# Uneven groups of tokens in a two-layer transformer kernel: groups of 8x6, 6, 6 and 4 units, with scatters, pieces and gathers set closer to each group's plan

## What is computed

```python
h = _layernorm(x) * (1 + ca) + sa
x = x + ga * attention(h)                  # 16 heads, softmax over 256 keys
h = _layernorm(x) * (1 + cb) + sb
topk_w, topk_i = jax.lax.top_k(h @ router_weight, 2)
# every token: only its two experts count
#   layer 0: act = (clip(up) + 1) * gate * sigmoid(1.702 * gate), with biases
#   layer 1: act = silu(h @ wg) * (h @ wu), plus a shared expert
x = x + gb * (w0 * expert_a(h) + w1 * expert_b(h))
```

## Time and profile before

| what | us |
|---|---|
| median of 3 runs | 1867.87 (1864.94 to 1874.45) |
| profiled execution, device time | 1869.03 |
| its span in the trace | 1867.3 |
| PE busy | 1491.6 |
| DVE busy | 1315.7 |
| ACT busy | 1157.5 |
| POOL busy | 1028.7 |

### The profile page before, as it was taken

One profiled execution on the slowest core, in us unless ns is written; L12 is line 12 of the kernel. 1 busy time (PEld: TensorE's weight loads), 2 busy tenths in 40 slices (PEclk: granted clock), 3 DMA queues, 4 the chain that ended last, 5 costly groups with the idle time before them and its releaser, 6 DMA issues.

```text
span 1867.3 us, 44529 instructions
## 1 busy us (share of the span) xinstructions
PE 1491.6 (80%) x13810; PEld 911.5 (49%) x13810; DVE 1315.7 (70%) x3981; ACT 1157.5 (62%) x2692; POOL 1028.7 (55%) x1411
## 2 busy tenths in 40 slices
PE   2779888889999888899999989998999887435540
PEld 1334444445555555555555555555555555435530
DVE  5669988978888877798888888887788765202110
ACT  1478877877777676677776767766776654113320
POOL 1223335634553766567764767565755556546736
PEclk9989999999999898899999999999999999667665
DMA  6774444445555554455554545555455433224432
GB/s 197 172 205 109 110 103 116 114 122 126 134 130 120 138 132 114 119 127 140 134 137 109 134 122 144 130 124 116 125 134 129 116 87 83 75 80 132 121 93 62
DMA packets 381606, 229.44 MB, mean 123 GB/s; under 512 B 28847, under 2 KB 370161, under 8 KB 380867
## 3 DMA queue, kind: packets, MB, share of 16 engines
q1 hardware_dynamic: 352675, 186.72, 41.4%
q0 software_dynamic: 16384, 33.59, 6.4%
q10 hardware_dynamic: 12320, 6.29, 1.2%
HBM read 122.44 MB, written 103.98 MB: 121 GB/s over the span
## 4 chain that ended last, share of the span: by engine, by line
PE 36%; POOL 20%; DVE 18%; issue 16%; another core or an unknown queue 4%; ACT 4%; DMA 2%; SPq 1%; POOLq 0%; DVEq 0%; ACTq 0%
DVE mx L1553 8%; PE ps_s L1161 7%; POOL y_in L642 7%; PE ps_job L1032 6%; PE ps_q L1020 3%; PE ps_q L1001 3%; POOL slot_dram L625 3%; PE ps_q L983 2%; POOL qk_part L669 2%; POOL y_two L677 2%; POOL qk_rest L665 2%; PE ps_job L1135 2%; PE ps_job L1127 2%; PE ps_q L1013 2%
## 5 line engine op out<-in xcount | busy, mean ns | idle before, releaser
L1553 DVE TENSOR_REDUCE mx<-ps_s 128x2 f32<-128x512 f32 x1024 | 688.2, 681 | 150.3 <-PE ps_s L1161 123.7
L821 ACT ACTIVATE prob<-ps_st 128x512 f32<-128x512 f32 x1024 | 598.9, 593 | 111.1 <-PE ps_st L1167 82.6
L1161 PE MATMUL ps_s<-k_stk,q_stk 51*128 51x256 bf16 x2048 | 403.4, 284 | 79.5 <-DVE mx L1553 37.2
L1167 PE MATMUL ps_st<-q_stk,k_stk 53*128 53x256 bf16 x2048 | 400.2, 281 | 0.8 <-ACT prob L821 0.8
L642 POOL DMA_INDIRECT y_in<-y_dram,slot x256 | 252.4, 986 | 106.7 <-issue 54.6
L1032 PE MATMUL ps_job<-prob,v_ext 128*32 128x256 f32 x4096 | 287.8, 400 | 25.6 <-issue 17.6
L625 POOL DMA_INDIRECT slot_dram<-h_row,slot x256 | 260.6, 1018 | 69.8 <-issue 65.1
L1161 PEld LDWEIGHTS ps_s<-k_stk,q_stk 51*128 51x128 bf16 x2048 | 118.3, 95 | 333.8 <-issue 182.7
L754 ACT ACTIVATE o_sb<-ps_job 128x256 f32<-128x256 f32 x256 | 97.1, 379 | 190.3 <-PE ps_job L1032 127.0
L1032 PEld LDWEIGHTS ps_job<-prob,v_ext 128*32 128x32 f32 x4096 | 115.1, 112 | 133.4 <-issue 54.4
L665 POOL TENSOR_TENSOR qk_rest<-qk_f,qk_part 128x512 f32<-128x512 f32 x64 | 73.9, 1154 | 187.3 <-ACT qk_part L852 187.3
(11 more groups left out here) (206 smaller groups left out, 2919.0 us busy)
## 6 DMA issues: line engine op xcount, KB each, us to landing
part_dram<-qk_part SPq DMA_DIRECT2D x128, 192.0 KB
q_stk<-part_dram SPq DMA_DIRECT2D x128, 192.0 KB
k_stk<-part_dram SPq DMA_DIRECT2D x128, 192.0 KB
...
part_dram<-qk_part SPq DMA_DIRECT2D x128, 128.0 KB
...
part_dram<-qk_part SPq DMA_DIRECT2D x128, 64.0 KB
```

Source lines behind the costliest of these rows:

```text
L821: sc.activation(prob[:, (k ^ 1) % 8, :], ps_st[k % 2][:], ACT.Exp).then_inc(exp_done, 1)
L1161: mm = pe.matmul(ps_s[j % 2][:, t * S:(t + 1) * S], q_stk[us.tri][r0:r0 + R_BIAS, hp, t * P:(t + 1) * P], k_stk[us.tri][r0:r0 + R_BIAS, hp ...
L1167: mm = pe.matmul(ps_st[k % 2][:, t * S:(t + 1) * S], k_stk[ut.tri][r1:r1 + R_MAX, hp, t * P:(t + 1) * P], q_stk[ut.tri][r1:r1 + R_MAX, hp, ...
L1553: dve.tensor_reduce(mx[:, hp // 4, :, 4 * par + hp % 4], ps_s[j % 2][:].rearrange("p (t s) -> p t s", s=S), AX_X, ALU.max).then_inc(max_do ...
```

## The change

- The units are split into groups of 8, 8, 8, 8, 8, 8, 6, 6 and 4 units. A group of 6 has 40 blocks (10 pieces), one of 4 has 32 (8 pieces): 100 pieces in all, not 96. There are 9 plans, not 8. The plan works on the group's own number of rows.
- The steps of scatters, pieces and gathers after a group's last unit change as in the table. Scatters and gathers of groups 0 to 4 take half as many steps as before.

| counted from | what | before | now |
|---|---|---|---|
| `last` | scatters of groups 0 to 5 | 91 to 181 | 92 to 138 |
| `last` | pieces of groups 0 to 4 | 195 to 312 | 147 to 264 |
| `last` | gathers of groups 0 to 4 (before: 0 to 4, one unit per 16 steps) | 332 to 450 | 286 to 348 |
| `END` | group 5: pieces, gathers | -61 to 56, 124 to 155 | -109 to -21, -2 to 36 |
| `END` | group 6: scatters, pieces, gathers | -37 to 53, 92 to 158, 176 to 207 | -68 to -34, -11 to 43, 58 to 81 |
| `END` | group 7: scatters, pieces, gathers | 91 to 122, 164 to 230, 248 to 279 | 31 to 54, 56 to 92, 107 to 130 |
| `END` | group 8: scatters, pieces, gathers | none | 90 to 105, 112 to 140, 152 to 167 |

- `slot_dram` has 3 buffers instead of 2. They are cleared by 18 DMAs of 512 KB, one every 10 steps from step 40 on, not by 2 of 3072 KB.
- Pieces of groups 6 to 8 (`quick`) go through their stages in 9 steps instead of 15.
- The gathers of groups 6 to 8 use four buffers: the two of `y_in` and two in the memory of `k_stk[0]`. Their gate rows come in two DMAs at `END+47` into the memory of `v_ext`, and DVE instead of POOL multiplies by them and adds to `x` (`add_rows`).

The core of the diff:

```diff
-G = 8
-NG = UNITS // G
-NB = G * S * 2 // P + E
+SIZES = [8] * 6 + [6, 6, 4]
+G = max(SIZES)
+NG = len(SIZES)
 QB = 4
+UNIT_AT = [sum(SIZES[:g]) for g in range(NG + 1)]
+BLOCKS = [size * S * 2 // P + E for size in SIZES]
+PIECES = [n // QB for n in BLOCKS]
 TAIL = NG - 2
+LATE = TAIL - 1
+RING = 4
...
-    for i in range(G):
+    for n in range(2 * TT * SIZES[g]):
+        SCATTER[last + 92 + n * 3 // 2 if late < 2 else END + (31, 90)[late - 2] + n] = (UNIT_AT[g] + n // 4, n % 4)
+    for i in range(PIECES[g]):
+        QUAD[last + 147 + 32 * (i // 3) + (0, 11, 21)[i % 3] if late < 0 else
+             END + (-109 + 8 * i, -11 + 6 * i, 56 + 4 * i, 112 + 4 * i)[late]] = PIECE_AT[g] + i
+    for i in range(SIZES[g]):
+        first = last + 286 + 8 * i if late < 0 else END + (-2 + 5 * i, 58 + 4 * i, 107 + 4 * i, 152 + 4 * i)[late]
+        apart, lag = (2, 13) if late < 0 else (1, 9)
         for j in range(2 * TT):
...
+STAGE = {"blocks": (0, 0), "gate_up": (3, 3), "clip": (3, 3), "tanh": (5, 3), "act": (6, 3), "product": (7, 7), "act_t": (10, 6),
+         "down": (15, 9), "store": (16, 10), "load": (-12, -5)}
...
+        y_rows = [y_in[0][:], y_in[1][:], spare[:, 0], spare[:, 1]]
+        gate_late = [v[:].rearrange("p t h v -> p (t h v)").rearrange("p (u d) -> p u d", d=D) for v in v_ext]
...
+                if step == END + 47:
+                    sp.wait_ge(av_mm, 4 * UNITS)
...
                     if u.no < 2:
                         pool.wait_ge(row_stored, 32)
+                    elif u.no < UNIT_AT[LATE] + 2:
+                        pool.wait_ge(y_summed, u.count(2, -2))
+                    elif u.no < UNIT_AT[LATE] + RING:
+                        pool.wait_ge(st_mm, S_DONE)
                     else:
-                        pool.wait_ge(y_summed, u.count(2, -2))
+                        pool.wait_ge(y_summed, u.count(2, 2 - 2 * RING))
...
-                if step == 40:
-                    clear_slots()
+                if step in range(40, 40 + 10 * 3 * CLEAR, 10):
+                    clear_slots(*divmod((step - 40) // 10, CLEAR))
...
+            def add_rows(u):
+
+                dve.wait_ge(y_summed, u.count(2, 2))
+                dve.wait_ge(gates_in, 32)
+                dve.wait_ge(sh_added, u.count1(1, 1))
+                i, j = divmod(u.no - UNIT_AT[LATE], 8)
+                dve.tensor_tensor(y_two[:], y_two[:], gate_late[i][:, j].rearrange("p (o d) -> p o d", o=1)
+                                  .broadcast_to([P, TT, D]), ALU.mult).then_inc(y_scaled, 1)
+                dve.wait_ge(y_scaled, u.count(1, 1))
+                dve.tensor_tensor(x[:, u.batch, :, :], x[:, u.batch, :, :], y_two[:], ALU.add).then_inc(y_added, 1)
```

More of the change, by code:

```diff
@@ L35 @@
 VW = 32
-G = 8
-NG = UNITS // G
-NB = G * S * 2 // P + E
+SIZES = [8] * 6 + [6, 6, 4]
+G = max(SIZES)
+NG = len(SIZES)
 QB = 4
-NQ = NB // QB
+UNIT_AT = [sum(SIZES[:g]) for g in range(NG + 1)]
+BLOCKS = [size * S * 2 // P + E for size in SIZES]
+NB = max(BLOCKS)
+PIECES = [n // QB for n in BLOCKS]
+PIECE_AT = [sum(PIECES[:g]) for g in range(NG + 1)]
+SECOND = UNIT_AT.index(B)
 TAIL = NG - 2
+LATE = TAIL - 1
+RING = 4
 LANES = 3
@@ L62, in __init__ @@
         self.batch = no - B * self.layer
-        self.group, self.slot = no // G, no % G
-        self.last = self.slot == G - 1
+        self.group = max(g for g in range(NG) if UNIT_AT[g] <= no)
+        self.slot = no - UNIT_AT[self.group]
+        self.last = no + 1 == UNIT_AT[self.group + 1]
     def count(self, per, c):
@@ L79, in __init__ @@
         self.no = no
-        self.group, self.i = no // NQ, no % NQ
-        self.layer = 0 if self.group < NG // 2 else 1
-        self.tail = self.group >= TAIL
-        first = TAIL * NQ
+        self.group = max(g for g in range(NG) if PIECE_AT[g] <= no)
+        self.i = no - PIECE_AT[self.group]
+        self.layer = 0 if self.group < SECOND else 1
+        self.quick, self.tail = self.group >= LATE, self.group >= TAIL
+        first = PIECE_AT[TAIL]
         self.par = no % 2
@@ L247, in build @@
         start_of = sb("start_of", [P, G * TT * 2])
-        slot = [sb(f"slot{i}", [P, G * TT * 2], U32) for i in range(NG)]
+        slot = [sb(f"slot{i}", [P, n * TT * 2], U32) for i, n in enumerate(SIZES)]
         over = sb("over", [NB, E])
@@ L310, in build @@
         zeros_in = sem("zeros_in")
-        slots_clear = sem("slots_clear")
+        slots_clear = [sem(f"slots_clear{i}") for i in range(3)]
         lanes_clear = sem("lanes_clear")
@@ L380, in act_done, with stored @@
             return (act0_ok, q.no + 1) if q.layer == 0 else (act_ok, q.count1(1))
+        def stored(g, n):
+            return (sum(PIECES[h] for h in range(g % 2, g, 2)) + n) * 16
         def y_freed(q):
@@ L505, in quad_store @@
                 sp.wait_ge(y_ok, q.no + 1)
+                if q.i == 0 and q.group >= 3:
+                    for par in range(2):
+                        sp.wait_ge(y_gathered[par], UNIT_AT[q.group - 2] // 2 * 64)
                 sp.dma_start(y_dram[q.group % 3].rearrange("(j p) d -> p j d", p=P)[:, q.i * QB:(q.i + 1) * QB, :],
@@ L527, in _ @@
                         max_rows(u, half)
-                q = quad_at(step, 16)
+                q = quad_at(step, "store")
                 if q:
                     quad_store(q)
-                q = quad_at(step, -12)
-                if q and q.i and not q.tail:
+                q = quad_at(step, "load")
+                if q and (q.i or q.quick):
                     quad_load(q)
-                q = quad_at(step, -5)
-                if q and (q.i == 0 or q.tail):
-                    quad_load(q)
+                if step + 6 in QUAD:
+                    q = Quad(QUAD[step + 6])
+                    if q.i == 0 and not q.quick:
+                        quad_load(q)
                 u = at(step, 44)
@@ L601, in count_seen @@
                     pool.wait_ge(rank_dn_mm, u.no)
-                    pool.wait_ge(seen_step, u.group * (G - 1) + u.slot)
+                    pool.wait_ge(seen_step, u.no - u.group)
                 if u.slot == 0:
@@ L673, in _ @@
                 u = done_at(step, 2)
-                if u:
+                if u and u.group < LATE:
                     pool.wait_ge(y_summed, u.count(2, 2))
@@ L1447, in plan @@
                 c = u.group * PLAN
+                n_blocks, n_rows = BLOCKS[u.group], SIZES[u.group] * TT * 2
+                mine, rows = hot_start[:, 0:n_rows, :], start_of[:, 0:n_rows]
                 if u.group:
@@ L1622, in _ @@
                     norm_rows(u)
-                if step == END + 66:
+                if step == END + 50:
                     dve.wait_ge(av_mm, 4 * UNITS)
@@ L1629, in _ @@
                     combine(u)
+                    if u.group >= LATE:
+                        add_rows(u)
 def kernel(**inputs):
```

150 lines of the change are left out of this document (81 added, 69 removed).

## The result

| | before | changed |
|---|---|---|
| median, us | 1867.7 (1864.94 to 1874.45) | 1822.0 (1816.94 to 1825.56) |
| ratio | | 0.9751, 95% interval 0.9719 to 0.9783 |
| span of the profiled execution | 1867.3 | 1820.1 |
| last unit begins (END) | 1494.5 | 1543.2 |
| last `slot` | 1603.7 | 1710.2 |

The account below looks back on a forecast made before the run. It took order stage by stage as the bound, chiefly the 263 us tail hanging on POOL's row of DMAs. END at 1531.5 (1494.5 - 7 + 26 + 28 - 10), then 151 and 99.5 us, gave 1782, forecast as 1783; range 1735 to 1840.

Parts of the forecast that it names:

- rival 2: Burst units lose 1 to 1.5 us each as scatters before `ln_rs` delay DVE: +40 to +55 us, 1820 to 1840; chance 0.2.
- clearing: ACT's queue: 18 small clears replace the big clear's 10.73 us hold; -7 us, bounds -11 and +2.
- END to last `slot`: From the last unit's start to the last plan: more pieces and a load wait, 151 us, bounds 109 and 170.
- after the last `slot`: Tail behind the last plan: scatters, gathers beside the last pieces, final gathers; 99.5 us instead of 263.4.
- last pieces stored: Tail: group 8's 8 pieces run beside group 7's gathers and are stored at 1749 us, last `slot` being at 1682.5.
- last 16 gathers to the end: End of the tail: 16 gathers at 1.25 us take 20 us, to 1769, then the end at 1782.
- Denser bursts: Main loop: scatters and gathers packed into fewer units load POOL like the earlier mix; -10 us.
- More pieces before END: Main loop: 74 pieces start before END, not 66; 8 x 3.2 = +26 us, bounds 16 and 34.
- the crowded place: END-68 to END-34: 24 scatters and 17 gathers need 70 us of POOL against 56 us of steps; 14 us more.
- the first (all hidden): Pieces and gathers moved ahead of END are hidden, gathers cost per unit: 1725 to 1755, say 1745 us; chance 0.2.
- The third: Slower: 2.5 us or more per burst unit over some 40 units, +100 us, about 1880; such units take 28.5; chance 0.05.
- The fourth (one `y_two`): Tail: late gathers' first rows wait for the sum before, pieces behind them on ACT; +24 us, 1806; chance 0.1.

Follow-up runs that it names:

- The loop's packing alone: Kernel before with only the changed main-loop tables for groups 0 to 4 (scatters of group 5 too): 1884.21 us, ratio 1.0092.
- the thinned kernel: Changed kernel with the gathers of group 4's last four units 32 steps later: 1811.67 us, ratio 0.9699 to the kernel before.
- the kernel with spread gathers: Changed kernel with the gathers of groups 0 to 3 spread again over one unit per 16 steps: 1873.13 us, ratio 1.0017 to the kernel before.

## Why the prediction came out as it did

The mechanism was right: what follows END shrinks by far more than the work moved ahead of it costs, 96 us against 49. Only about half of the forecast gain came. The time lies in the range given because its upper part was there for rival 2, not because the sum held: the bursts, the stretch from END to `slot` and the last pieces all took longer than put. Two of the signs failed as well: POOL was not busy without a gap from END to END+54 (it waits 14.25 us at 1566), and 109.9 us follow the last `slot`, not under 105. The sizes, against the slower chip's traces:

| term | predicted | measured |
|---|---|---|
| clearing | -7 | -10.7 at unit 3; -10.6 alone |
| END | +37 | +48.7 |
| END to last `slot` | 151 | 167.0 (147.7 on the faster chip) |
| after the last `slot` | 99.5 | 109.9 (96.4) |
| of it, last pieces stored | 66.5 | 84 (70) |
| last 16 gathers to the end | 33 | 26 |

**Clearing.** Right in kind; the 18 issues that I priced at 3.7 us cost nothing that unit 3 or the total shows (0.37 us each in ACT's queue).

**Denser bursts, the term of -10 us.** This is the first step that failed. I took a unit's time from the average number of DMAs, and both ends of the range from units with the mix of before. The loop's packing alone gave +33 at END, where my terms for its share (18 x 1.28 - 10) give +13: the packing added 10 us where I had taken 10 off. The price isn't one per DMA nor one per unit. In the units of layer 1, some 10 DMAs cost little, and the eight beyond cost 0.6 to 1 us each in the mean. I looked at this once, for END-68 to END-34, and priced it at 14 us; the place took 16 more than before, and moving 16 gathers away gives 17 back on the faster chip. So that term was right in size, and the error lies in the -10 that I set against it.

**More pieces before END.** +26 was priced. What the packed loop and the clears leave of +48.7 is 48.7 - 33.3 + 10.7 = 26 us for 8 pieces, 2 more gathers and the crowded place together. My sum without the clears is +44, and less the 13 of the packed loop it leaves 31 for them. So these were priced 5 us too dear, and the clears' gain of 10.7 us was put 4 us too low. The miss of 12 us at END is the 20 us of the bursts less these two. How the 26 us fall on pieces and the crowded place no run on this chip shows; with 8 us for the place (the thinned kernel here) to 17 (on the faster chip) and 2.6 for the gathers, the pieces cost 6 to 15, under their lower bound of 16.

**END to `slot`.** The sum of 151 lies 3 us above the faster chip's 147.7 and 16 below the slower one's. PE's wait for group 7's load was put at 6 us; it is 9.06 us here:

```profile
1654.41 1.11 PE L1033 MATMUL ps_q<-ident,h_blk 128*128 128x128 f32 x4 [9.06 <-DMA h_blk<-slot_dram]
```

The pieces were over-counted. I priced 3 + 9 more of them between END and `slot`, but 9 is what stands in the second part by the tables, and some stood there before. In the traces PE transposes 18 pieces between END and the last `slot`, against 8 before, so 10 more; at 4.2 us each that is 8 us off the sum, which makes it 143. It is thus 5 us short even of the faster chip, and that 151 came near 147.7 is in part luck. The 19 us between the two chips probably come from waits of the kind shown in the next section, which the trace of before showed too and which I didn't price: I took durations of rows, and left out the waits that no row explains. What they cost on the path is not shown one by one.

**After the last `slot`.** The 16 scatters took 20.3 us as predicted. The pieces came 17 us later than the sum (4 later on the faster chip), so the rhythm of 4.22 us of the earlier trace rows held about on the one chip and not on the other. The end was 7 us shorter than put: from the start of the last gather (1813.37 us) 6.7 us follow, not 12.8. That is likely because no backlog of sums stands there now; no run isolates it.

**Rivals.** Of the first (all hidden) there is no sign. The second (bursts bind) holds in part: not in 40 units, but in units 59 and 60, and it would have taken all the gain if gathers and scatters had overlapped in the loop, as the kernel with spread gathers shows for the slower chip. The third didn't come: units 53 to 55 with their 29 scatters take 30.5, 24.6 and 27.0 us, 27.4 in the mean, and 28.5 was its limit. The fourth (one `y_two`) is seen in two waits of POOL for DVE's sums, 14.25 us at 1566 and 8.08 at 1764 (on the faster chip 7.32 at 1507 and none over 4 later). Two buffers instead of four cost 1 to 5 us, and another order of the sums nothing that shows, which speaks against it; a second `y_two` was not tried. The time of 1822 us falls into the band of the second rival by number; END at 1543 lies below its mark of 1570.

One reading of rows was loose: by the earlier trace rows PE is busy 90 and 94% of the first two stretches, not 91 to 94. Nothing in the sum hangs on it.

The rule of the Trainium skill ("SBUF — State Buffer", Who interferes with whom) on the port pair that VectorE and POOL share was to make a burst up to 10 us longer. A scatter takes 1001 ns in the mean here against 1018 before, so denser bursts don't make the single DMA longer; no run here isolates the port.

## What to carry to other kernels

Moving DMAs ahead of a critical point is cheap as long as the issuing engine's own row still fits into each stretch. So count per stretch, not in the mean: here about 10 indirect DMAs a unit were nearly free and the eight beyond cost 0.6 to 1 us each. Two moves that each lose alone (packed scatters +1.7%, packed gathers +1.2%) lost less together, most likely because they then no longer met. Where an engine waits 9 us on the path, look for what would be late next before taking the wait away: 5 us less waiting for the load came back as 5 us more for DVE.

A number in a step table orders only its own engine's row. Before running such an edit, check which row really changes.

## What the chip showed beyond the plan

The same program takes 1822 us on one chip and 1735 us on another, and the kernel before 1868 and 1777: 5%. POOL's scatters have nearly the same mean on both (1001 and 997 ns). The page's line of the faster run, against the one above:

```profile
PE 1471.5 (85%) x13909; PEld 901.5 (52%) x13909; DVE 1343.8 (77%) x4032; ACT 1177.1 (68%) x2708; POOL 1001.7 (58%) x1376
```

PE has 34 us less on record, at a mean granted clock of 0.941 against 0.921. The other thing that differs is waits without a recorded reason, which the waits view puts down to "remote" or "issue". In the changed kernel's trace on the slower chip the remote ones come to 118 us (112 in the kernel before, 101 to 180 in the other four), in all eight traces of the faster chips to 0 (sums over all engines, which overlap). "Remote" means that a semaphore was counted up and no instruction's recorded end stands near. Every one of these waits is of an instruction of ACT or DVE that reads what PE wrote. Rows of the slower chip's changed kernel; columns: what waited and for what, us in total, times, longest.

```profile
ACT o_sb L807 <- remote: 41.9, 16, 5.2
...
DVE mx L1619 <- remote: 24.5, 9, 5.0
...
DVE prob L1560 <- issue: 25.4, 3, 22.2
```

The clearest place is the start of the last group's pieces. On the slower chip ACT's rows, and PE's rows beside them:

```profile
1736.66 0.60 ACT L828 ACTIVATE prob<-ps_q 128x512 f32<-128x512 f32 x1 [17.17 <-issue]
...
1752.72 0.60 ACT L828 ACTIVATE prob<-ps_s 128x512 f32<-128x512 f32 x1 [10.05 <-issue]
1761.12 0.60 ACT L847 ACTIVATE prob<-ps_q 128x512 f32<-128x512 f32 x1 [7.81 <-remote]
```

```profile
1735.51 1.12 PE L1033 MATMUL ps_q<-ident,h_blk 128*128 128x128 f32 x4 [17.34 <-DMA h_blk<-slot_dram]
...
1739.25 1.06 PE L1033 MATMUL ps_s<-ident,q_stk 128*128 128x128 f32 x4
1743.63 1.11 PE L1063 MATMUL ps_q<-ident,prob 128*128 128x128 f32 x4 [3.32 <-issue]
```

and the same instructions on the faster one:

```profile
1664.74 0.60 ACT L828 ACTIVATE prob<-ps_q 128x512 f32<-128x512 f32 x1 [17.58 <-PE ps_q L1033]
...
1668.42 0.60 ACT L828 ACTIVATE prob<-ps_s 128x512 f32<-128x512 f32 x1 [0.41 <-PE ps_s L1033]
1669.68 0.60 ACT L847 ACTIVATE prob<-ps_q 128x512 f32<-128x512 f32 x1 [0.66 <-PE ps_q L1063]
```

```profile
1663.58 1.12 PE L1033 MATMUL ps_q<-ident,h_blk 128*128 128x128 f32 x4 [16.91 <-DMA h_blk<-slot_dram]
...
1667.33 1.06 PE L1033 MATMUL ps_s<-ident,q_stk 128*128 128x128 f32 x4
1668.98 0.66 PE L1063 MATMUL ps_q<-ident,prob 128*128 128x128 f32 x4 [0.59 <-DVE prob L1565]
```

ACT copies what PE's L1033 wrote. On the slower chip the record lets that matmul end at 1740.3 us, and ACT starts at 1752.72; on the faster one it ends at 1668.39 and the copy starts at 1668.42. From the first transposes to L847's copy it is 25.6 us against 6.1. For L847's copy the trace tells more: the semaphore that L1063 counts up when it is done was counted up at 1761.10 us, 16 us after that matmul's recorded end (1743.63 + 1.11 us). On both chips the same unbroken row of POOL's DMAs stands beside this. So the ends of matmuls, which are modelled, can be over 10 us too early where PE is held up, and then a wait says "issue" or "remote". For L828's copy at 1752.72 us the trace has no such count, so there it stays open whether PE or ACT was late. What holds PE up on that chip no run here shows.
